# Second token block's mean square and the first two reciprocal roots on GpSimd, in a fused feed-forward and adapter kernel on one core

## What is computed

```
scale = cond @ norm_w.T + 1.0
ms = mean(x * x, axis=-1)
h = x * (scale[:, None, :] * rsqrt(ms + 1e-6))
u = h @ up_w.T                      # 2 x 2048 rows: val and gate
val, gate = split(u, 2)
h = val * gelu(gate)                # exact gelu
y = act_quant(h) @ weight_quant(down_w).T + x
Wd_b = Wd + (cond @ Wdd.T + bdd) * 0.1     # adapter weights from the condition
Wu_b = Wu + (cond @ Wdu.T + bdu) * 0.1
out = y + relu(y @ Wd_b + bd) @ Wu_b + bu
```

## Time and profile before

| | |
|---|---|
| median of 3 runs | 839.31 us (838.85 to 839.36) |
| the profiled execution: its own time | 840.44 us |
| the profiled execution: span from first to last instruction | 838.7 us |
| PE busy | 821.2 us, 98% of the span |
| DVE busy | 664.3 us, 79% |
| ACT busy | 399.8 us, 48% |
| POOL busy | 121.3 us, 14% |

### The profile page before, as it was taken

How to read it: one execution, slowest core, us unless ns; L and a number is a source line. 1 busy time by engine, 2 the same in 40 slices (tenths; PEclk the granted TensorE clock), 3 DMA queues, 4 the chain that set the end, 5 groups by cost and what they waited for, 6 DMA issues and landing times.

```text
span 838.7 us, 11856 instructions
## 1 busy us (share of the span) xinstructions
PE 821.2 (98%) x3914; PEld 359.4 (43%) x3914; DVE 664.3 (79%) x968; ACT 399.8 (48%) x653; POOL 121.3 (14%) x91
## 2 busy tenths in 40 slices
PE   5999999999999999999999999999999999999998
PEld 4334444444344334444444444444444444444443
DVE  5998787889878889767787678988986586675986
ACT  5778887776454532227445543326433333324000
POOL 0363332302001153300101011100200000001000
PEclk9999999999999999999999999999999999999999
DMA  9879989666899862377798865337247435435232
GB/s 343 338 257 347 343 289 297 233 217 226 303 347 366 330 218 95 136 271 272 280 326 303 304 223 191 116 95 255 72 137 239 138 95 189 138 95 176 101 125 76
DMA packets 64860, 186.65 MB, mean 223 GB/s; under 512 B 7072, under 2 KB 8352, under 8 KB 64416
## 3 DMA queue, kind: packets, MB, share of 16 engines
q1 hardware_dynamic: 64512, 185.63, 63.5%
q10 hardware_dynamic: 288, 0.26, 0.1%
HBM read 154.41 MB, written 30.41 MB: 220 GB/s over the span
## 4 chain that ended last, share of the span: by engine, by line
PE 85%; DVE 5%; issue 3%; ACT 1%; DVEq 0%; ACTq 0%
PE b_ps L1351 9%; PE b_ps L1355 9%; PE b_ps L1353 9%; PE aux_ps L1406 6%; PE a_ps L1351 6%; PE aux_ps L1464 6%; PE a_ps L1355 6%; PE a_ps L1353 6%; PE c_ps L1351 3%; PE aux_ps L1542 3%; PE e_ps L1351 3%; PE e_ps L1355 3%; PE e_ps L1353 3%; PE c_ps L1353 3%; PE c_ps L1355 3%
## 5 line engine op out<-in xcount | busy, mean ns | idle before, releaser
L1954 DVE SCALAR_TENSOR_TENSOR h_ring<-v_sb,unscale,gelu 128x512 f32<-128x512 f32 x63 | 55.5, 881 | 58.0 <-ACT gelu L1092 31.9
L1351 PE MATMUL b_ps<-t_mov,u_l 128*128 128x512 f16 x252 | 95.5, 379 | 3.8 <-DVE c_ps L1915 3.6
L1355 PE MATMUL b_ps<-t_mov,u_l 128*128 128x512 f16 x252 | 95.5, 379 | 0.0
L1353 PE MATMUL b_ps<-t_mov,u_l 128*128 128x512 f16 x252 | 95.5, 379 | 0.0
L1978 DVE TENSOR_TENSOR hmax<-gelu,hmax 128x512 f32<-128x512 f32 x120 | 88.6, 740 | 7.8 <-ACT gelu L1098 2.9
L1068 ACT ACTIVATE b_ps<-a_ps 128x512 f32<-128x512 f32 x63 | 36.7, 582 | 94.1 <-PE a_ps L1355 93.9
L1102 ACT ACTIVATE gelu<-h_ring 128x512 f32<-128x512 f32 x64 | 40.3, 629 | 67.6 <-DVE h_ring L1954 67.6
L2013 DVE TENSOR_TENSOR h_ring<-h_ring,qscale 128x1024 f16<-128x1024 f32 x48 | 64.7, 1387 | 0.0
L1084 ACT ACTIVATE gelu<-a_ps,unscale 128x512 f32<-128x512 f32 x64 | 43.7, 682 | 43.3 <-DVE hmax L1978 41.1
L916 POOL PARTITION_ALL_REDUCE yscale<-hmax x8 | 17.9, 2266 | 321.0 <-DVE hmax L1978 320.3
L1098 ACT ACTIVATE gelu<-h_ring 128x512 f32<-128x512 f32 x64 | 40.2, 628 | 45.6 <-DVE h_ring L1964 45.3
(11 more groups left out here) (264 smaller groups left out, 1701.4 us busy)
## 6 DMA issues: line engine op xcount, KB each, us to landing
w_ring<-in_Wdu SPq DMA_DIRECT2D x64, 512.0 KB, 6.0
w_ring<-in_Wdd SPq DMA_DIRECT2D x56, 512.0 KB, 7.2
u_l<-ul_dram SPq DMA_DIRECT2D x48, 512.0 KB, 4.7
u_e<-ue_dram SPq DMA_DIRECT2D x48, 384.0 KB, 3.2
h_ring<-in_up_w SPq DMA_DIRECT2D x16, 512.0 KB, 6.4
x_sb<-in_x SPq DMA_DIRECT2D x8, 1024.0 KB, 7.9
res<-in_down_w SPq DMA_DIRECT2D x16, 512.0 KB, 7.1
ul_dram<-u_l SPq DMA_DIRECT2D x15, 512.0 KB, 5.6
```

The costliest lines, as they stand in the source:

```text
L1351: pe.matmul(ps[:, :], weight(n, p, 0, k), hi, start=fresh and k == 0, stop=False, skip_group_check=True)
L1353: pe.matmul(ps[:, :], weight(n, p, 0, k), lo, start=False, stop=False, skip_group_check=True)
L1355: mm = pe.matmul(ps[:, :], weight(n, p, 1, k), hi, start=False, stop=k == 1, skip_group_check=True)
L1954: dve.scalar_tensor_tensor(out=h_slot(n)[:, TB:TS], in0=val[:, :], scalar=unscale[:, s // 2, j:j + 1], in1=gelu2[:, :], op0=ALU.mult, op1= ...
```

## The change

It does six things.

1. Block 1's squares now go to the second halves (columns 512 to 1023) of `h_ring` slots 0 to 3. DVE adds them in two pairs and then once more to a single sum (`second_sum_squares(2)`), and GpSimd's `partition_all_reduce` sums it over the partitions. `stat1` is gone from PE. `mean_square(1)` takes the total's diagonal on DVE: a multiply by the identity and a reduction.
2. The two `rsqrt` calls of blocks 0 and 1 (20 DVE instructions) are replaced by `first_roots(t)` on GpSimd, one `tensor_tensor` of 128x4 with the operation pow and a tile `power` of -0.5.
3. The first two products (`a_ps[0]` and `b_ps[0]` on B11) are interleaved, so that their matmuls stand in the order in which operands come: the four high by high, then weight low for `a_ps`, token low for both, weight low for `b_ps`.
4. On ACT `t_high(0, B21)` stands ahead of `row_sums(2)` and `stage_group(0)`. `stage_group(1)` and what follows wait for both roots.
5. On DVE `x_scaled(0, (2, 3))` and `u_low(0, 2)` stand ahead of `mean_square(1)`.
6. The loads of adapter weights 8 to 11 no longer wait for block 1's sums; PE no longer waits for `s_ms` ahead of the bounds of quads 1 and 2.

```diff
+            def first_roots(t):
+                pool.wait_ge(s_ms, t + 1)
+                cols = slice(NT * t, NT * t + NT)
+                pool.tensor_tensor(rs[:, 0, cols], ms[:, cols], power[:, :], ALU.pow)\
+                    .then_inc(s_rs, 1)
-            pool.wait_ge(s_rs, 2)
+            first_roots(0)
+            pool.wait_ge(s_sq1, 3)
+            pool.partition_all_reduce(first_total, first_squares1[0], P, AR.add)\
+                .then_inc(s_stat1, 1)
+            first_roots(1)
             for j in SUM_ORDER:
                 weight_sums(j)
...
             def mean_square(i):
                 if i == 1:
-                    dve.wait_ge(s_stat1, 2)
+                    dve.wait_ge(s_stat1, 1)
+                    dve.wait_ge(s_const, 4)
                     total = ms_half[:, col:col + NT]
-                    link(dve.tensor_reduce(
-                        total, e_ps[:, 0:2 * NT].rearrange("p (k t) -> p t k", k=2),
-                        AX_X, ALU.add))
+                    link(dve.tensor_tensor(first_grid, first_grid, diagonal, ALU.mult))
+                    link(dve.tensor_reduce(total, first_grid, AX_X, ALU.add))
...
             condition()
             second_sum_squares(0)
             mean_square(0)
-            rsqrt(0)
             aux_ready(dve, "total", 0)
             exponents(0, 0, bank("total", 0))
             first_scales()
             second_sum_squares(1)
             x_scaled(0, (0, 1))
             u_low(0, 0)
+            second_sum_squares(2)
             t_low(0, B11)
             first_val_low()
             second_scales()
-            mean_square(1)
-            rsqrt(1)
             x_scaled(0, (2, 3))
             u_low(0, 2)
+            dve.wait_ge(s_table, 1)
+            mean_square(1)
             t_low(0, B21)
             x_scaled(1)
...
             stat(0)
-            stat1(0)
             first_bounds()
-            pe.wait_ge(s_const, 3)
+            pe.wait_ge(s_const, 4)
             spread_rs(0)
-            stat1(1)
-            first_product(a_ps[0], True, False, B11).then_inc(s_p[1], 1)
-            first_product(b_ps[0], True, True, B11).then_inc(s_p[5], 1)
+            gate, val = first_operands(True, False, B11), first_operands(True, True, B11)
+            pe.wait_ge(s_uhi, part_count(0, 0))
+            pe.wait_ge(s_first_row, 1)
+            for k in range(2):
+                if k:
+                    pe.wait_ge(s_thi, 1)
+                pe.matmul(a_ps[0][:, :], gate[0](0, k), gate[1](0, k), start=(k == 0),
+                          stop=False, skip_group_check=True)
+            pe.wait_ge(s_first_hi, 1)
...
             adapter_group(0)
             spread_rs(1)
...
             adapter_group(3)
-            pe.wait_ge(s_ms, 2)
             bounds(1, 2, e_ps).then_inc(s_total, 1)
...
             u_high(0, 2)
+            t_high(0, B21)
             row_sums(2)
             stage_group(0)
-            t_high(0, B21)
+            act.wait_ge(s_rs, 2)
             stage_group(1)
...
                 if n in EARLY_SLOT:
-                    if n >= 8:
-                        sp.wait_ge(s_stat1, 2)
                     sp.dma_start(w_tile(n), src[n]).then_inc(s_w_early[n], 16)
```

More of the change, by code:

```diff
@@ L315, in build @@
         aux_ps = [ctx.enter_context(nc.psum_tensor(f"aux_ps{n}", [P, TB], F32)) for n in range(2)]
+        first_squares1 = [h_ring[:, k, TB:TS] for k in range(KD)]
+        first_total = h_ring[:, 2, TB:TS]
+        first_grid = first_total.rearrange("p (t q) -> p t q", t=NT)
         def bank(*key):
@@ L873, in _ @@
             pool.memset(ident[:, :], 1.0).then_inc(s_const, 1)
-            pool.wait_ge(s_const, 2)
+            pool.memset(power[:, :], -0.5).then_inc(s_const, 1)
+            pool.wait_ge(s_const, 3)
             pool.affine_select(out=ident[:, :], in_=ident[:, :], compare_op=ALU.is_equal, fill=0.0,
@@ L1357, in product, with first_operands @@
                 mm.then_inc(s_p[p], 1)
[L1359 to L1364, removed]
+            def first_operands(first_half, val, m):
                 def rows(part, k):
@@ L1374, in split, with first_product @@
                     return t_mov[:, PLACE[m], part, TB * k:TB * k + TB]
-                if m == B11:
-                    pe.wait_ge(s_first_row, 1)
-                else:
-                    pe.wait_ge(s_thi, split_count(0, m))
+                return rows, split
+            def first_product(ps, first_half, val, m):
+                rows, split = first_operands(first_half, val, m)
+                if first_half and val:
+                    pe.wait_ge(s_first_hi, 1)
+                else:
+                    pe.wait_ge(s_uhi, part_count(0, 0 if first_half else 2))
+                pe.wait_ge(s_thi, split_count(0, m))
                 for k in range(2):
-                    if m == B11 and k == 1:
-                        pe.wait_ge(s_thi, 1)
                     pe.matmul(ps[:, :], rows(0, k), split(0, k), start=first_half and k == 0,
@@ L1422, in stat @@
                 mm.then_inc(s_stat if i else s_aux, 1)
[L1424 to L1432, removed]
             def spread_rs(i):
@@ L1578, in _ @@
             stat(0)
-            stat1(0)
             first_bounds()
-            pe.wait_ge(s_const, 3)
+            pe.wait_ge(s_const, 4)
             spread_rs(0)
-            stat1(1)
-            first_product(a_ps[0], True, False, B11).then_inc(s_p[1], 1)
-            first_product(b_ps[0], True, True, B11).then_inc(s_p[5], 1)
+            gate, val = first_operands(True, False, B11), first_operands(True, True, B11)
[6 more added lines that the diff above has]
+                          stop=False, skip_group_check=True)
+            pe.wait_ge(s_first_hi, 1)
+            for k in range(2):
+                pe.matmul(b_ps[0][:, :], val[0](0, k), val[1](0, k), start=(k == 0),
+                          stop=False, skip_group_check=True)
+            pe.wait_ge(s_ulo, part_count(0, 0))
+            for k in range(2):
+                pe.matmul(a_ps[0][:, :], gate[0](1, k), gate[1](0, k), start=False,
+                          stop=False, skip_group_check=True)
+            pe.wait_ge(s_tlo, split_count(0, B11))
+            for k in range(2):
+                mm = pe.matmul(a_ps[0][:, :], gate[0](0, k), gate[1](1, k), start=False,
+                               stop=(k == 1), skip_group_check=True)
+            mm.then_inc(s_p[1], 1)
+            for k in range(2):
+                pe.matmul(b_ps[0][:, :], val[0](0, k), val[1](1, k), start=False,
+                          stop=False, skip_group_check=True)
+            pe.wait_ge(s_first_lo, 1)
+            for k in range(2):
+                mm = pe.matmul(b_ps[0][:, :], val[0](1, k), val[1](0, k), start=False,
+                               stop=(k == 1), skip_group_check=True)
+            mm.then_inc(s_p[5], 1)
             adapter_group(0)
@@ L1794, in second_sum_squares @@
             def second_sum_squares(part):
[L1796 to L1799, removed]
+                if part < 2:
+                    dve.wait_ge(s_sq, KD + 2 * part + 2)
+                    a, b = first_squares1[2 * part:2 * part + 2]
+                else:
+                    dve.wait_ge(s_sq1, 2)
+                    a, b = first_squares1[0], first_squares1[2]
+                dve.tensor_tensor(a, a, b, ALU.add).then_inc(s_sq1, 1)
             def mean_square(i):
@@ L1823, in mean_square, with rsqrt @@
                                   ALU.mult, ALU.add).then_inc(s_ms, 1)
[L1825 to L1833, removed]
+            def rsqrt(i):
+                dve.wait_ge(s_ms, i + 2)
+                a, half, t = ms[:, :], ms_half[:, :], rs_t[:, :]
+                y = rs[:, (i // 2) % 2, :]
                 link(dve.tensor_scalar(half, a, -0.5, None, ALU.mult))
```

8 lines of the change are left out of this document (5 added, 3 removed).

## The result

The changed kernel takes 852.88 us (median of 6 runs, 851.41 to 854.06) where the kernel before takes 839.38 us (6 runs beside it, 838.85 to 840.02): 13.5 us more, a ratio of 1.0164 with a 95% interval of 1.0153 to 1.0174. The profiled execution has a time of 853.46 us and a span of 851.7 us, 13.0 us over the span before.

A forecast was written before the change was run, and what follows sets the result against it. PE was taken to bind, with DVE nearly full up to 60 us. PE's 12.9 + 1.3 - 2.4 = 11.8 us and DVE's 10.4 gave +11.5: 851.9 profiled, 850.8 us median, range 844.3 to 857.

The forecast's parts named there:

- Root 0: Block 0's root by GpSimd's pow, taken at 0.3 us: ready at 12.3 us, 1.4 us early.
- First set-up: GpSimd's loading of the reduction's code after block 0's root: 8.0 us, to 20.3.
- Second set-up: GpSimd's loading of elementwise code between the all-reduce and block 1's pow: 10.3 us, to 34.7.
- All-reduce: GpSimd's sum of block 1's squares over partitions: 4.1 us, to 24.4.
- Root 1: Block 1's root by pow on GpSimd: ready at 35.0 us against 22.10, its spread on PE 12.9 us late.
- The rival of two short loads: About 6 us for each GpSimd code load: chain ends at 28.7, time 844.5 us; no chance of its own.
- Adapter group 0: PE through the first product and this group by about 20.5 us, then idle 14 us at the spread.
- PE's slow phase: PE starting slowly after the pause, half of 2.5 us wasted: +1.3 us.
- Given back: PE's idle time before 60 us repaying delay, as DVE is now ahead: up to 2.4 us.
- quiet set-ups: Rival: GpSimd's code loads served ahead of bulk transfers, 844.3 to about 847 us; chance 0.22.
- hidden set-ups: Rival: GpSimd's code loads cost nothing here, block 1's x scaled 1.3 us early, 838.0 us; chance 0.04.
- Worse than quoted: Rival: each code load over 10.4 us behind full DMA queues, or nothing repaid; 855 to 860 us; chance 0.18.

The follow-up runs named there:

- quiet_loads: The changed kernel with SP holding back all loads behind adapter weight 1 until both roots are ready; 855.33 us in one run.
- small_reduce: The changed kernel with block 1's sum over partitions on PE and an unneeded 128x4 all-reduce between the two roots; 851.41 us in one run.
- pe_kept_busy: The changed kernel with 58 extra matmuls on PE filling the pause ahead of the spread of block 1's root; 850.57 us.
- groups_ahead: The changed kernel with adapter groups 1 and 2 ahead of the spread of block 1's root on PE; 851.95 us.
- no_reduce: The kernel before with pow roots, interleaved products and moved t_high and x_scaled, no all-reduce, stat1 kept on PE; 839.25 us, ratio 0.9991.
- pow_roots: The kernel before with only its two rsqrt calls replaced by GpSimd's pow; 839.37 us, ratio 0.9995.
- root1_by_dve: The changed kernel with block 1's root by DVE's ten instructions, the all-reduce still on GpSimd; 848.13 us, ratio 1.0091.

## Why the prediction was right

The forecast of 850.8 us lies 2.1 us below the measured 852.88; direction, mechanism and place were right: two set-ups of GpSimd's code on the way of block 1's root, and PE standing still behind them. In the sum 11.5 us were taken and the spans differ by 13.0; the other 0.5 us are the step from the profiled execution to the median, put at 1.1 us from the kernel before and 0.6 in the changed one. By its steps:

- **Root 0** was put at 12.3 and came at 12.79. Pow was taken at 0.3 us with 0.7 as the upper bound; it takes 1.05 us for 128x4 elements, above that bound. The nearest rows were a memset and an addition, and neither was near.
- **First set-up**: 8.0 us, measured 9.13. **Second set-up**: 10.3, measured 8.53. Together 18.3 against 17.66. The two errors cancel. That the price rises with the DMA load was right in direction (quiet_loads), but the load does not fix it: at a DMA share of 0.96 to 1.03 the elementwise code took 8.07 to 8.53 us in four kernels and 10.53 in small_reduce, and the reduction's code took 5.86 us at a share of 0.00 and 5.93 at 0.38, so between these two nothing rises.
- **All-reduce**: 4.1, measured 3.25. I took the row on summed squares while the 3.25 us of the other all-reduces proved to be its length.
- **Root 1**: 35.0, measured 12.79 + 9.13 + 3.25 + 8.53 + 1.05 = 34.75. That these agree within 0.25 us is in part luck, since five errors of 0.5 to 1.8 us cancel. The spread is 12.35 us late against 12.9. The DVE steps under the second set-up were hidden as said.
- **The rival of two short loads**: with 6 us for each set-up the sum was 844.5, 8.4 us too low. The Trainium skill's GPSIMD Engine Reference, section Instruction dispatch, gives about 6 us for the first call of freshly loaded code. This case agrees for the reduction's code alone and only where the DMA engines are little loaded (5.86, 5.93, and 6.13 us in quiet_loads); the elementwise code took 7.11 even at a DMA share of 0.00, and under full load the two took 8.07 to 10.53.
- **Adapter group 0** was put at about 20.5 for its end and ended at 21.44, although the first product started 1.84 us early and not 0.7 to 0.8; behind that PE ran its products at half rate for nearly 4 us, where the prediction had 2.5. It decides nothing, as the prediction said, since the root was late.
- **PE's slow phase** is one of two terms that were mis-sized: 1.3 us forecast, from a phase of 2.5 us at the start; measured 4.62 - 2.44 = 2.18 us, since here the half rate lasts from 34.81 to past 39.43. pe_kept_busy shows that about 2 us reach the end.
- **Given back** is the other: 2.4 us forecast, from all of PE's idle time before 60 us; measured 14.63 - 13.00 = 1.6 us, 1.1 of them in that stretch. The wrong step is that DVE's lead gives all of this idle time back. Of the 2.33 us of waits 0.75 were for ACT, and behind the change that wait is 1.35 us. ACT's late `stage_group` is not the reason. The half-rate adapter groups do come late to ACT, its high parts of block 1's operands start only at 40.05, and DVE waits 2.45 us for them; but in pe_kept_busy, where DVE waits 0.73 us there, and in groups_ahead, where it doesn't wait, the same 1.1 us come back. From the first product on B21 to quad 1 the shift grows by 0.1 us only, so the claim that ACT's part "costs nothing of its own" held. That PE is busy all the time from 60 us on was read from rows that end at 80 us. PE still waits later, 1.65 us at 311 us in the kernel before, and 0.5 us came back in such places, half of it because GpSimd idled 0.29 us less far from the change (last section).

With 12.35 + 2.18 - 1.6 the sum is 12.9 us, against 13.0 in the spans. Against the forecast's 12.9 + 1.3 - 2.4 the spread takes 0.55 us off and the two mis-sized terms put 0.9 and 0.8 us on. Of the rivals, quiet set-ups fell by the two rows of 9.13 and 8.53 us, and the hidden set-ups by the same rows: POOL waits for nothing else there. Worse than quoted did not come either: neither set-up is over 10.4 us, and something is given back. What the change was to gain is small: no_reduce holds nearly all of it and comes out even.

## What to carry to other kernels

Before a step goes to GpSimd, look at what kind of code its neighbours in that engine's list use: one all-reduce between elementwise instructions costs two set-ups, here 6 to 10.5 us each, and shows in no diff, only in the engine's list and as idle time that ends with "issue". Price it under the DMA load of its own stretch. And count a long pause of TensorE twice: once for its length, and once for the half rate behind it, here 2.2 us. Idle time of an engine gives a delay back only if what it waits for comes from an engine that the delay has put ahead: look at each wait's releaser before counting it.

## What the runs showed of the hardware that was not expected

- A pow of 128x4 on GpSimd takes 1.05 us (1.01 to 1.45 over all runs), more than an addition of 128x256 (0.71 to 0.74 us).
- After the pause the granted clock reads 0.50 and matmuls of 512 columns run at half rate; at the start of the program they run at half rate too while it reads 1.00. So the start's half rate can only be read from the distances between matmuls.
- An early shift of the whole program does not reach the end unchanged, whichever its sign: between quads 22 and 27 the shifts of the table move by -0.6 to +2.3 us. For groups_ahead, where 1.6 us are lost at quad 23, the row shows the transfer that is in the way. The step of quad 26 goes back to idle time of GpSimd ahead of its `down_sums`. Before:

```profile
305.85 3.82 POOL L949 TENSOR_TENSOR w_ring<-wq 128x2048 fp8e4<-128x2048 fp8e4 x1 [10.27 <-issue]
306.26 3.96 DVE L1954 SCALAR_TENSOR_TENSOR h_ring<-v_sb,unscale,gelu 128x512 f32<-128x512 f32 x1 [1.89 <-issue]
```

and in pow_roots:

```profile
304.77 3.82 POOL L959 TENSOR_TENSOR w_ring<-wq 128x2048 fp8e4<-128x2048 fp8e4 x1 [9.66 <-issue]
305.79 3.35 DVE L1964 SCALAR_TENSOR_TENSOR h_ring<-v_sb,unscale,gelu 128x512 f32<-128x512 f32 x1 [1.89 <-issue]
```

DVE's instruction takes 0.74 us in the quad before, at 295.60. Here it ends 0.55 us behind the end of GpSimd's, in both kernels and, to 0.02 us, in each of the others of the table, and PE waits for what DVE does next (1.65 us before, 1.03 in pow_roots). So the length of GpSimd's idle time there, 9.66 to 10.77 us over these kernels with no edit near it, sets when PE goes on; the trace gives it as "issue", a set-up, though it may hold a wait for data too. The 0.61 us by which it is shorter in pow_roots are the 0.61 us that this kernel gains at quad 27, and the 0.29 us of the changed kernel (9.98) are its first late step. No run tested what holds DVE. Open as well are 1.7 us more that root1_by_dve loses in quad 26, no_reduce's 0.27 us at quad 23, and the changed kernel's second step, 0.29 us at quad 45.
